# A vision transformer layer on one core: the quantised rows made bf16 before they are transposed

## What is computed

```python
def activation_quant(x):
    scale = 127.0 / jnp.maximum(jnp.max(jnp.abs(x), axis=-1, keepdims=True), EPS_Q)
    return jnp.clip(jnp.round(x * scale), -128, 127) / scale
def bitlinear(x, w, g):
    x_norm = rmsnorm(x, g)
    x_q = x_norm + stop_gradient(activation_quant(x_norm) - x_norm)
    w_q = w + stop_gradient(weight_quant(w) - w)      # ternary: -1, 0, 1 over a scale
    return jnp.einsum('bsd,od->bso', x_q, w_q)
h = bitlinear(x, w_in, g_in); up, gate = jnp.split(h, 2, axis=-1)
return bitlinear(jax.nn.silu(gate) * up, w_out, g_out)
```

## Time and profile before

| | us |
|---|---|
| median of three runs | 1444.98 |
| profiled execution, its own time | 1452.2 |
| its span, first to last instruction | 1450.4 |
| PE busy, share of the span | 1392.3 (96%) |
| DVE busy | 977.9 (67%) |
| ACT busy | 894.0 (62%) |
| POOL busy | 880.3 (61%) |
| the 396 transposes of yr (L552), PE busy | 64.1 |
| the 198 transposes of xr (L533), PE busy | 43.5 |
| DVE idle until max_scores (L450) | 186.0 |
| mean granted TensorE clock, share of 2.4 GHz | 0.957 |

### The profile page before, as it was taken

The page is one execution under the profiler, slowest core; times in us unless marked ns, Lnnn a source line. Parts: engine busy times, 40 slices in busy tenths (PEclk is TensorE's granted clock), DMA queues, the critical chain, the costliest instruction groups (busy, mean ns, idle before and its releaser), DMA issues.

```text
span 1450.4 us, 40381 instructions
## 1 busy us (share of the span) xinstructions
PE 1392.3 (96%) x14658; PEld 1005.6 (69%) x14658; DVE 977.9 (67%) x2322; ACT 894.0 (62%) x1606; POOL 880.3 (61%) x1609
## 2 busy tenths in 40 slices
PE   5899999999999999999999999999999999999985
PEld 4566777777777777777777777777777777776553
DVE  1545676777777677777677777677777767775556
ACT  1335566666666666666666666666666666665464
POOL 4544676666666666666676666666666666665234
PEclk9869999999999999999999999999999999998586
DMA  5201111221212221121221121122121212100000
GB/s 163 74 25 45 48 40 42 61 54 49 56 36 56 53 55 39 50 63 34 53 53 43 47 53 48 39 61 54 50 54 36 57 51 55 40 13 10 7 9 22
DMA packets 125615, 68.84 MB, mean 47 GB/s; under 512 B 49985, under 2 KB 124846, under 8 KB 125326
## 3 DMA queue, kind: packets, MB, share of 16 engines
q1 hardware_dynamic: 124348, 63.46, 16.8%
q10 hardware_dynamic: 1074, 2.80, 0.7%
HBM read 56.50 MB, written 9.73 MB: 46 GB/s over the span
## 4 chain that ended last, share of the span: by engine, by line
PE 92%; DVE 3%; issue 1%; SPq 1%; ACT 1%; POOL 0%; DMA 0%; POOLq 0%; ACTq 0%; DVEq 0%
PE turn L408 14%; PE turn L499 11%; PE turn L427 10%; PE score L476 9%; PE turn L544 7%; PE turn L487 6%; PE turn L437 5%; PE score L472 5%; PE score L450 5%; PE turn L525 4%; PE turn L552 3%; PE turn L508 3%; PE turn L533 2%; PE turn L526 2%; PE turn L562 2%; PE turn L518 1%
## 5 line engine op out<-in xcount | busy, mean ns | idle before, releaser
L846 DVE TENSOR_REDUCE nmax<-score 99x8 f32<-99x1584 f32 x192 | 347.0, 1807 | 186.0 <-PE score L450 186.0
L658 ACT ACTIVATE prob<-score 99x1584 f32<-99x1584 f32 x192 | 286.5, 1492 | 115.5 <-PE score L476 115.5
L996 POOL TENSOR_TENSOR ropec<-qk,rope 128x384 f32<-128x384 f32 x99 | 99.0, 1000 | 237.5 <-ACT qk L636 235.5
L408 PE MATMUL turn<-wlin,xp 128*128 128x192 f32 x1188 | 227.2, 343 | 15.2 <-DMA xp<-in_x 13.7
L408 PEld LDWEIGHTS turn<-wlin,xp 128*128 128x128 f32 x1188 | 198.2, 196 | 27.2 <-issue 17.2
L476 PE MATMUL score<-qkT 16*99 16x198 f32 x3072 | 185.5, 333 | 0.0
L499 PE MATMUL turn<-prob,vaug 99*32 99x198 f32 x3072 | 176.1, 349 | 0.0
L427 PE MATMUL turn<-wqkv,xT 96*128 96x384 f32 x396 | 156.3, 518 | 1.8 <-ACT xT L628 1.8
L472 PE MATMUL score<-nmaxT,onehot 3*99 3x198 f32 x1536 | 145.5, 367 | 10.8 <-DVE nmax L846 10.3
L1026 POOL TENSOR_TENSOR yg<-y,gout 128x512 f32<-128x512 f32 x99 | 126.0, 1272 | 40.5 <-ACT yr L720 40.5
L628 ACT ACTIVATE xT<-turn 96x256 f32<-96x256 f32 x99 | 37.6, 380 | 167.0 <-PE turn L418 167.0
(11 more groups left out here) (98 smaller groups left out, 2810.9 us busy)
## 6 DMA issues: line engine op xcount, KB each, us to landing
xp<-in_x SPq DMA_DIRECT2D x64, 588.0 KB, 5.2
out<-h SPq DMA_DIRECT2D x99, 96.0 KB, 1.7
bias<-in_added SPq DMA_DIRECT2D x30, 74.2 KB
win<-in_win ACTq DMA_DIRECT2D x1, 768.0 KB
wlin<-in_wlin ACTq DMA_DIRECT2D x1, 576.0 KB, 3.9
rope<-in_cos SPq DMA_DIRECT2D x30, 6.2 KB
rope<-in_sin SPq DMA_DIRECT2D x30, 6.2 KB
wqkv<-in_wqkv ACTq DMA_DIRECT2D x1, 432.0 KB
```

The source lines that it names most:

```text
L408: last = pe.matmul(turn[:, k, 0:D], xp[:, c, place:place + TILE], wlin[:, c, :], start=(c == 0), stop=(c == KC - 1))
L658: act.activation(prob[:, :, 4 * g:4 * g + 4, :].rearrange("p t r n -> p r t n"), score[0:TT, :, 0:2 * TOKENS].rearrange("p r (t n) -> p r ...
L846: dve.tensor_reduce(nmax[:, b % 2, :, :].rearrange("p t (r j) -> p r t j", r=4)[:, :, :, g], score[0:TT, :, 0:2 * TOKENS].rearrange("p r ( ...
L996: pool.tensor_tensor(ropec[:, :].rearrange("p (h e f) -> p h e f", e=DH // 2, f=2), src, cos, ALU.mult)\
```

## The change

round_x and round_y still write xr and yr in fp32 with MAGIC. Two new DVE instructions take MAGIC off and write the whole numbers as bf16 into new tiles xi and yi: whole_x on 128 x 192 and whole_y on 128 x 512. PE transposes xi and yi against a bf16 identity into the same banks of turn, which are read and written there as bf16. ACT's evacuations copy bf16 to bf16 without a bias. round_x and round_y now wait for the DVE pass of two tiles back instead of the transpose of two tiles back. The two new functions stand in DVE's step behind row_max(2s) and ahead of finish, whole_y of tile at(PROJ_AT, s - 5) first. The number of banks, `take` and PE's order stay as they are.

```diff
+        identb = sb("identb", [128, 128], BF16)
+        xi = sb("xi", [128, 2, D], BF16)
+        yi = sb("yi", [128, 2, FF], BF16)
+        turnb = turn[:, :, :].bitcast(BF16)
...
             def transpose_xr(i):
-                pe.wait_ge(xr_ready, i + 1)
+                if i == 0:
+                    pe.wait_ge(ident_ready, 1)
+                pe.wait_ge(xi_ready, i + 1)
                 k = take(("xiT", i), 1, xiT_copied, i + 1)
                 for c in range(2):
-                    last = pe.transpose(turn[0:DC, k, c * TILE:(c + 1) * TILE], xr[:, i % 2, c * DC:(c + 1) * DC],
-                                        ident[:, :])
+                    last = pe.transpose(turnb[0:DC, k, c * TILE:(c + 1) * TILE], xi[:, i % 2, c * DC:(c + 1) * DC],
+                                        identb[:, :])
...
             def transpose_yr(i):
-                pe.wait_ge(yr_ready, i + 1)
+                pe.wait_ge(yi_ready, i + 1)
                 k = take(("yiT", i), 1, yiT_copied, i + 1)
                 for c in range(FC):
-                    last = pe.transpose(turn[:, k, c * TILE:(c + 1) * TILE], yr[:, i % 2, c * 128:(c + 1) * 128],
-                                        ident[:, :])
+                    last = pe.transpose(turnb[:, k, c * TILE:(c + 1) * TILE], yi[:, i % 2, c * 128:(c + 1) * 128],
+                                        identb[:, :])
...
-                act.activation(yiT[:, i % 2, :, :], turn[:, bank_of["yiT", i], :].rearrange("p (c n) -> p c n", c=FC), ACT.Copy,
-                               bias=-MAGIC).then_inc(yiT_copied, 1)
+                act.activation(yiT[:, i % 2, :, :], turnb[:, bank_of["yiT", i], 0:FF].rearrange("p (c n) -> p c n", c=FC),
+                               ACT.Copy).then_inc(yiT_copied, 1)
...
+                dve.tensor_copy(identb[:, :], ident[:, :]).then_inc(ident_ready, 1)
...
+            def whole_x(i):
+                dve.wait_ge(xr_ready, i + 1)
+                if i >= 2:
+                    dve.wait_ge(xiT_ready, i - 1)
+                dve.tensor_scalar(xi[:, i % 2, :], xr[:, i % 2, :], MAGIC, None, ALU.subtract).then_inc(xi_ready, 1)
+
+            def whole_y(i):
+                dve.wait_ge(yr_ready, i + 1)
+                if i >= 2:
+                    dve.wait_ge(yiT_ready, i - 1)
+                dve.tensor_scalar(yi[:, i % 2, :], yr[:, i % 2, :], MAGIC, None, ALU.subtract).then_inc(yi_ready, 1)
...
                 for n in at(MAX_AT, 2 * s):
                     row_max(n)
+                for i in at(PROJ_AT, s - 5):
+                    whole_y(i)
+                for i in at(PROJ_AT, s - 2):
+                    whole_x(i)
                 for i in at(PROJ_AT, s - 6):
                     finish(i)
```

More of the change, by code:

```diff
@@ L278, in build @@
         xr_ready = sem("xr_ready")
+        xi_ready = sem("xi_ready")
+        yi_ready = sem("yi_ready")
+        ident_ready = sem("ident_ready")
         xiT_ready = sem("xiT_ready")
@@ L690, in copy_xiT @@
                     act.wait_ge(ffin_ready, i - TBUF + 1)
-                act.activation(xiT[:, i % TBUF, :, :], turn[0:DC, bank_of["xiT", i], 0:2 * TILE].rearrange("p (c n) -> p c n", c=2),
-                               ACT.Copy, bias=-MAGIC).then_inc(xiT_copied, 1)
+                act.activation(xiT[:, i % TBUF, :, :], turnb[0:DC, bank_of["xiT", i], 0:2 * TILE].rearrange("p (c n) -> p c n", c=2),
+                               ACT.Copy).then_inc(xiT_copied, 1)
             def tanh_gate(i):
@@ L711, in round_x @@
                 if i >= 2:
-                    act.wait_ge(xiT_ready, i - 1)
+                    act.wait_ge(xi_ready, i - 1)
                 act.activation(xr[:, i % 2, :], u[:, i % TBUF, :], ACT.Copy, scale=sx[:, i % TBUF:i % TBUF + 1],
@@ L718, in round_y @@
                 if i >= 2:
-                    act.wait_ge(yiT_ready, i - 1)
+                    act.wait_ge(yi_ready, i - 1)
                 act.activation(yr[:, i % 2, :], yg[:, i % 2, :], ACT.Copy, scale=sy[:, i % TBUF:i % TBUF + 1],
```

## The result

The changed kernel took 1529.97 us (median of four runs, 1509.6 to 1534.5) against 1444.9 us. The ratio is 1.050, with a 95% interval of 1.040 to 1.060. It is 5% slower. The forecast was 1470 us with a range up to 1482, so the sign was right, and the size was wrong by 60 us, outside the range. The execution profiled is the longest of the four, 1534.5 us for a span of 1532.7; the spans of the others were 1531.8, 1524.5 and 1507.8 us, at mean granted clocks of 0.904, 0.910 and 0.919, against 0.904 in the one profiled.

The account below looks back on a forecast made before the run. PE was taken as the bound in the middle. 1452.2 less 29 for the transposes, plus 29, 20 and 5 for lost time, gave 1477; less 7.2 for the median, 1470 us, range 1420 to 1482.

Parts of the forecast that it names:

- the sum: Whole run: profiled time less PE's gain plus PE's losses, 1452.2 - 29 + 29 + 20 + 5 = 1477 us.
- The first kind of step: Steps where transpose_xn takes finish's bank: finish 1.61 us late, PE loses 1.16 us, 25 times, 29 us.
- The second kind, project_out: Steps where project_out takes finish's bank: finish 2.15 us late, PE loses 0.76 us, 26 times, 20 us.
- DVE claimed ahead: Rival: a pass without an open wait takes its turn during row_max, so whole_y is never late; 1443 us, chance 0.17.
- both passes went as a pair: Rival: whole_x follows whole_y without letting POOL in; 1424 us, 1.5% faster, chance 0.33.
- POOL went in between: Likeliest case: the held POOL instruction runs between whole_y and whole_x, making finish late; 1470 us, chance 0.45.
- The third kind, weigh_values: Steps where weigh_values takes finish's bank: finish 1.34 us late against a cover of 2.00 us, nothing lost.
- The gain: PE's bf16 transposes: 0.054 us saved each, 0.32 us a tile over some 90 tiles, 29 us off.
- The end: Last steps: whole_x behind POOL delays DVE's chain about 1 us in some five steps, 5 us (0 to 8).

Follow-up runs that it names:

- spread: Changed kernel with whole_x moved ahead of residual and whole_y behind gain_x: 1448.0 us, ratio 1.001.
- passes_only: Changed kernel with both passes in place but their output unused, the transposes reading xr and yr in fp32: 1521.3 us, ratio 1.049.
- stall_long: Kernel before plus an unused DVE maximum over 1520 elements ahead of finish in steps 10 to 99, no new pass: 1549.4 us.
- stall_short: Kernel before plus an unused DVE maximum over 860 elements ahead of finish in steps 10 to 99, no new pass: 1470.4 us, ratio 1.020.
- after_finish: Changed kernel with finish moved ahead of both passes, which then stand right behind it: 1486.1 us, ratio 1.017.
- y_short: Changed kernel with whole_y over 192 of its 512 columns, the second product left out for the other 320: 1490.6 us.
- x_first: Changed kernel with the two passes swapped, whole_x ahead of whole_y, both still ahead of finish: 1444.4 us, ratio 0.990.
- halfword: Kernel before with no DVE pass: 17152 added to MAGIC, PE transposes low half-words as bf16, ACT takes 17152 off: 1435.7 us, ratio 0.986.
- y_only: Changed kernel with whole_x left out and the xr path kept fp32: 1445.96 us, ratio 0.996.
- x_only: Changed kernel with whole_y left out and the yr path kept fp32: 1437.5 us, ratio 0.997.

## Why the prediction was wrong

A ledger of the middle, from embed(15) to embed(95), in us. Pauses are PE's gaps over 0.2 us between 120 and 1300 us beyond the 3.4 of before. The clock's part is half the time at the lower level between embed(15) and embed(95). The gain is spread's 19.7, where the transposes are bf16.

| kernel | pauses | clock | gain | sum | measured |
|---|---|---|---|---|---|
| changed | 25.6 | 63.2 | -19.7 | 69.1 | 66.0 |
| passes_only | 25.5 | 32.4 | 0 | 57.9 | 59.2 |
| stall_long | 40.8 | 37.5 | 0 | 78.3 | 80.8 |
| stall_short | 13.4 | 0 | 0 | 13.4 | 16.8 |
| after_finish | 27.8 | 11.9 | -19.7 | 20.0 | 21.9 |
| y_short | 23.9 | 18.8 | -19.7 | 23.0 | 20.9 |
| x_first | 3.9 | 6.8 | -19.7 | -9.0 | -7.7 |

The rows close within 4 us. The clock falls behind some 8 of 24 like pauses, for 3.4 us at one time and 20.5 at another. In x_first, with no pause over 0.8 us, it fell twice: there five times a pause of 0.77 us was followed within 2 us by one of 0.57, and a fall came behind two of the five. In after_finish the two falls came 1.0 and 2.0 us behind the end of a pause of 1.0 us, of which it has five. I can't say what makes it fall behind one pause and not another.

- **The step that failed is the sum**, which took every lost microsecond at its own price and held the clock at the 1.00 of the earlier trace rows. The forecast had 49 us of PE pauses in it and never asked what they do to the clock. 27 of them came, and the clock took another 63. No rival had it either. That alone is more than the miss of 60. stall_long shows that such pauses bring the clock down by themselves.
- **The first kind of step**: right. finish 1.60 late for 1.61, 24 pauses of 1.1 for 25 of 1.16: 26.7 us for 29.
- **The second kind, project_out**: wrong, 20 us forecast and 0 found. Here DVE claimed ahead, as in that rival, and then both passes went as a pair, as in the other one, while in the first kind POOL went in between, as the forecast had it. I had let one case hold for all steps. Its row was there: L820 ahead of L1003.
- **The third kind, weigh_values**: right, nothing lost.
- **The gain**: right in mechanism. The distance fell from 0.109 to 0.057 us; the run kept 0.25 (spread) to 0.28 us a tile (halfword) of the 0.32 forecast. The Trainium skill's 81 ns (TensorE: Matmul & The Clock Gate, Back-to-back issue gap) would have given 6 x (0.109 - 0.081) = 0.17, and the trace disagrees.
- **The end**: 5 us forecast, 16.7 found behind embed(98) (160.4 for 143.7). whole_x stands on the chain with 1.3 us, step after step, at half the clock. Of the chain that ended last:

```profile
1488.78 0.62 ACT yr L729
...
1489.77 1.32 DVE xi L907
...
1497.18 0.62 ACT yr L729
```

Its steps are 8.4 us long. I had priced whole_x's delay in five steps, and it was late in ten. How much of the 16.7 is the clock and how much the passes is not settled. Beside before's 143.7, spread, whose steps are as long, has 156.7; y_only, without whole_x, 156.2; x_first, where whole_x takes 0.25 us and a step 7.1, 147.1; x_only loses nothing. These are single traces, and the runs of the kernel before alone spread over 29 us (1432.2 to 1461.4).

With the clock held, the other errors would have come near to cancelling (20 us too many in the second kind, against a gain 9 too large and an end 12 too small): 1452.2 - 19.7 + 25.6 + 16.7 = 1475. That is close to the forecast's 1477, but by luck.

## What to carry to other kernels

Where PE is busy for nearly all the time, a pause that recurs can have two prices: its own length, and the half-speed stretches behind it. Those cost 0.9 to 2.5 times as much again in the three kernels with pauses of 1.1 us or more, 0.4 and 0.8 times in the two with pauses of up to 1.0 us, and nothing where single pauses stayed at 0.5; in x_first 3.9 us of shorter pauses, some in close pairs, cost another 6.8. Ask of any work put ahead of an instruction that frees a PE buffer how long PE will pause. Two DVE passes beside a busy POOL are worth trying in both orders and in other places: the order alone was worth 74 us of the middle here, and 6% of the whole (1.050 against 0.990).

## What the runs showed of the hardware that I had not expected

- Pauses of 1.1 us in a PE stream that was busy 97% of the time brought the clock from 2.4 to 1.2 GHz for 3 to 20 us at a time, in all 23 cases of three kernels 1.5 to 2.6 us behind the end of such a pause; pauses of 0.48 us in the same places never did.
- A POOL instruction that began up to 1.6 us ahead of a DVE pass stood still until the pass was over (L1024 2.82 us in place of 1.00), where the pass came right behind row_max and its input had been ready before POOL's instruction began.
- bf16 transposes with a weight load each stood 0.057 us apart also where their input was every second half-word (halfword).
